# Pacing row gathers by the landing of earlier ones instead of by memsets

## The reference

```python
# 1  edge sum over the weighted edges, then a linear layer
agg = segment_sum(f[src] * w[:, None], dst);  x += agg @ W.T + b
# 2  top-1 routing to 8 experts (relu feed-forward, capacity per expert)
# 3  linear layer first, then the edge sum over the same edges turned around
h = f @ W;  agg = segment_sum(w[:, None] * h[dst], src)
x += relu(batch_norm(agg + bias) * gamma + beta)
# 4  graph attention with 4 heads over the second edge list gives scores of
#    4 experts per node; top-2 softmax mixes 4 gelu feed-forward experts
alpha = segment_softmax(leaky_relu(a_src[src] + a_dst[dst]), dst)
scores = layer_norm(segment_sum(h[src] * alpha, dst) + b_gat).mean(heads)
```

## Time and profile before

| | |
|---|---|
| three runs | 8183.62, 8189.40, 8189.93 us; median 8189.4 |
| profiled execution | span 8556.1 us, first to last instruction; no time outside the span is given for it |
| busy share of the span | PE 67%, DVE 53%, ACT 44%, POOL 68% |
| DMA | 797.56 MB, 93 GB/s over the span |
| gathers of POOL | 1563 + 1563 + 1122 in the three parts |

### The profile page before, as it was taken

The page is one execution under the profiler, slowest core; times in us unless marked ns, Lnnn a source line. Parts: engine busy times, 40 slices in busy tenths (PEclk is TensorE's granted clock), DMA queues, the critical chain, the costliest instruction groups (busy, mean ns, idle before and its releaser), DMA issues. The chain is left out here.

```text
span 8556.1 us, 91570 instructions
## 1 busy us (share of the span) xinstructions
PE 5764.1 (67%) x19687; PEld 3851.9 (45%) x19687; DVE 4500.6 (53%) x8804; ACT 3777.5 (44%) x9645; POOL 5818.2 (68%) x7545
## 2 busy tenths in 40 slices
PE   5454555555556999968465656565556888888866
PEld 4333333333335666644243434443333555555545
DVE  5354555545456999958454454554457222222227
ACT  5555555655554222226355555555555222222213
POOL 3666666666644222226688888888886688888875
PEclk8677767676665999989666767766678999999988
DMA  7333333333332111126333333333333322222218
GB/s 227 91 90 89 90 91 91 92 91 91 91 116 81 45 50 49 46 65 206 99 90 91 91 89 91 88 91 90 88 91 129 95 59 57 56 58 55 56 47 324
DMA packets 498681, 797.56 MB, mean 93 GB/s; under 512 B 121278, under 2 KB 363563, under 8 KB 498059
## 3 DMA queue, kind: packets, MB, share of 16 engines
q0 software_dynamic: 200256, 453.47, 19.5%
q1 hardware_dynamic: 297904, 338.22, 12.2%
HBM read 595.60 MB, written 197.30 MB: 93 GB/s over the span
## 5 line engine op out<-in xcount | busy, mean ns | idle before, releaser
L1013 PE MATMUL part<-rows,spread 128*128 x6656 | 2481.5, 527 | 1990.5 <-issue 984.0
L1013 PEld LDWEIGHTS part<-rows,spread 128*128 128x128 f32 x6656 | 1613.8, 261 | 2797.6 <-issue 2539.6
L970 DVE TENSOR_TENSOR agg<-agg,part 128x257 f32 (+1 forms) x3328 | 1405.1, 422 | 2230.5 <-PE part L1013 721.7
L953 POOL DMA_INDIRECT rows<-f,row x1563 | 1549.6, 991 | 733.8 <-issue 453.0
L1037 ACT ACTIVATE spread<-iota,place 128x128 f32<-128x128 f32 x3328 | 1016.1, 387 | 2038.2 <-PE part L1013 1309.5
L953 POOL DMA_INDIRECT rows<-h,row x1563 | 1550.5, 992 | 258.4 <-issue 256.3
L1952 POOL DMA_INDIRECT rows<-gat,src x1122 | 1077.9, 961 | 185.0 <-issue 185.0
L1043 ACT ACTIVATE spread<-spread,weight 128x128 f32<-128x128 f32 x3328 | 1017.5, 388 | 14.1 <-ACT spread L1039 0.3
L2030 PE MATMUL y_ps<-agg,hid 128*128 128x256 f32 x3136 | 765.4, 405 | 190.7 <-DVE y_all L2160 190.7
L2030 PEld LDWEIGHTS y_ps<-agg,hid 128*128 128x128 f32 x3136 | 640.9, 206 | 342.2 <-DVE y_all L2160 209.5
L404 POOL COPY spare<-pay 128x1024 f32<-128x1024 f32 x105 | 222.3, 2117 | 735.7 <-DVE pay L391 505.7
(11 more groups left out here) (400 smaller groups left out, 6449.2 us busy)
## 6 DMA issues: line engine op xcount, KB each, us to landing
expert_rows<-y_all SPq DMA_DIRECT2D x196, 256.0 KB
made<-expert_rows SPq DMA_DIRECT2D x49, 1024.0 KB
x<-x SPq DMA_DIRECT2D x42, 896.0 KB
rows<-f,row POOLq DMA_INDIRECT x1563
rows<-h,row POOLq DMA_INDIRECT x1563
rows<-gat,src POOLq DMA_INDIRECT x1122
xbuf<-zero SPq DMA_DIRECT2D x16, 1024.0 KB
x<-xbuf SPq DMA_DIRECT2D x32, 512.0 KB
```

The lines of the kernel that those rows point to most:

```text
L953: pool.indirect_dma_start(out=rows[:, u, 0:D], out_offset=None, in_=table, in_offset=bass.IndirectOffsetOnAxis(ap=q.row[:, i:i + 1], axis= ...
L970: nc.vector.tensor_tensor(sum_t, sum_t, part[:, p % NB, 0:WIDE], ALU.add).then_inc(added, 1)
L1013: nc.tensor.matmul(part[:, p % NB, 0:WIDE], spread[:, p % (2 * BANKS), :], row_p, start=True, stop=True).then_inc(multiplied, 1)
```

## The change

A new constant, `AFLOAT = 3`. In both edge sums the memsets and their semaphore go, and from gather 3 on each gather waits until the third gather ahead of it has landed. In the attention the memsets go as well; a gather's semaphore is now chosen by its number, `gathered[i % 3]`, a gather waits for the landing of the one three ahead, and DVE, before a block, waits on all three semaphores. The waits for `freed` stay.

```diff
+AFLOAT = 3
@@ aggregate_edges
-        worded, rested = s.sem("worded"), s.sem("rested")
+        worded = s.sem("worded")
@@
                     if i >= SPAN and u % BANKS == 0:
                         pool.wait_ge(freed, (i - SPAN) // BANKS + 1)
-                    if not begun:
-                        if i:
-                            pool.wait_ge(rested, i)
-                        nc.gpsimd.memset(k.zero[:, 0:3 * P // 2], 0.0).then_inc(rested, 1)
+                    if i >= AFLOAT:
+                        pool.wait_ge(gathered[(i - AFLOAT) % SPAN], (i - AFLOAT) // SPAN * 16 + 16)
                     pool.indirect_dma_start(out=rows[:, u, 0:D], ...)
@@ attend
-        gathered = [s.sem(f"gathered{n}") for n in range(3)]
+        gathered = [s.sem(f"gathered{n}") for n in range(AFLOAT)]
@@
                     for j in range(B):
+                        i = b * B + j
+                        if i >= AFLOAT:
+                            pool.wait_ge(gathered[i % AFLOAT], i // AFLOAT * 16)
                         pool.indirect_dma_start(out=rows[b % 3][:, j, :], out_offset=None, in_=table,
-                                                in_offset=at(src[:, b * B + j:b * B + j + 1])).then_inc(gathered[b % 3], 16)
-                        if b or j:
-                            pool.wait_ge(rested, b * B + j)
-                        nc.gpsimd.memset(rest[:, :], 0.0).then_inc(rested, 1)
+                                                in_offset=at(src[:, i:i + 1])).then_inc(gathered[i % AFLOAT], 16)
@@
-                    dve.wait_ge(gathered[b % 3], (b // 3 + 1) * B * 16)
+                    for n in range(AFLOAT):
+                        dve.wait_ge(gathered[n], len(range(n, (b + 1) * B, AFLOAT)) * 16)
```

More of the change, by code:

```diff
@@ L1909, in attend @@
         fix_i, spot_i = s.sb("fix_i", [P, 1], I32), s.sb("spot_i", [P, 1], I32)
-        begun, rest = s.sb("begun", [P, GROWS], F32), s.sb("rest", [P, 2 * P], F32)
+        begun = s.sb("begun", [P, GROWS], F32)
         rows = [s.sb(f"rows{n}", [P, B, GROWS], F32) for n in range(3)]
@@ L1933, in attend @@
         ft_in, y_out = [s.sem(f"ft_in{h}") for h in range(2)], [s.sem(f"y_out{h}") for h in range(3)]
-        gathered = [s.sem(f"gathered{n}") for n in range(3)]
+        gathered = [s.sem(f"gathered{n}") for n in range(AFLOAT)]
         stored = [s.sem(f"stored{n}") for n in range(2)]
-        spared, rested = s.sem("spared"), s.sem("rested")
+        spared = s.sem("spared")
         own, chain, freed, shifted, exped, made, tail_done, tail_turned, tail_exp, tail_exped, joined_done, carried, row_in, row_exp, row_exped, row_done, row_out = (
```

## The result

The changed kernel takes 7860.93 us (median of 4 runs, 7856.37 to 7864.25) against 8189.15 us for the kernel before, measured beside it (4 runs, 8183.62 to 8189.93): a ratio of 0.9597, 95% interval 0.9585 to 0.9609, or 328 us less. The direction was forecast.

A forecast was written before the change was run, and what follows sets the result against it. POOL's gathers were taken to bind the attention, and PE, ACT and DVE both edge sums. 8556.1 - 217 = 8339 us profiled; from the 8189.4 us runs, 7972 whole or 7981 scaled, so 7975, range 7930 to 8220.

The forecast's parts named there:

- Without interruption 1563 of them would take 1954: First edge sum: gathers at a pitch of 1.25 us would take 1954 us of a stretch of 2275.
- Step 1: Attention: memsets between gathers go, pitch falls from 1.4545 to 1.261 us, gain 217 us, at most 284.
- step 3: All three stretches: 4239 waits for the landing three gathers ahead, taken to cost 0.
- Step 2: Second edge sum: memsets go, POOL saves 216 us of time in which it ran ahead; gain taken as 0, at most 30.
- A stretched gather doesn't change that: Landing waits: a long gather delays its successors on POOL as much as itself, so landings stay some 1.25 us old.
- landings come late, and the loop of three sets the pitch: Rival, new waits of edge sums and attention: pitch 1.50 us at 4.5 us per loop, 161 us slower, 8350; 16%.
- The rule against it: Landing waits: the skill page's 2 us HBM latency at high load would make a landing 4.3 us, so waits bind.
- Step 4: Attention: DVE waits on three semaphores a block instead of one, 66 more waits; covered, or 1 us if uncovered.
- More: the second edge sum follows too: Rival: gathers bind in the second edge sum without the profiler; 30 us more gain, at most some 90, 7880 to 7945; 6%.

The follow-up runs named there:

- the second trace: The kernel before, unchanged, profiled a second time: 8190.52 us, span 8188.8 us.

## Why the prediction was wrong, step by step

**What bounds the kernel.** The reading of the attention was right, that of the edge sums wrong. "So both edge sums run at the pace of PE, ACT and DVE" rests on the earlier trace rows, which show the disturbed execution alone, and of PE's wait only the part that its records could name (51.6 us there, 1725.1 in the second trace). "Without interruption 1563 of them would take 1954" took the median gather of 0.946 us; their mean is 0.999 us, and with the 0.304 between them that gives the 2037 us of the undisturbed first sum.

**Step 1, memsets of the attention: right.** Forecast 217 us; alone, with its landing waits, this part gave 183, and without waits the stage shrank from 1629 to 1405, 224 us. The pitch after a bare gather is (1063.6 + 341.9) / 1122 = 1.253 us, against the 1.261 forecast. With waits it is 1.289 (1068.9 + 377.9): the missing 36 us belong to step 3. PE's stalls on y_ps fell to 58.3 / 33 = 1.8 us a block (forecast 2), DVE's wait to 472.1 / 33 = 14.3 us a block (forecast 12). POOL still sets the period, 1447 / 33 = 43.8 us.

**Step 2, memsets of the second edge sum: the step that failed.** "I take 0", with at most 30 us of gain. The working of the price was right: 1563 x (0.274 + 0.164 - 0.300) = 216 us, and the stage lost 2238 - 2041 = 197 without waits. What was wrong was "but of time in which it ran ahead": in the undisturbed execution no gather of this sum waits for a free bank, and PE waits for the rows. POOL's own lines had it: the "2236 of 2305 us" that the prediction added up for POOL and gave to a rival match the 2238 us that the stage takes undisturbed. So POOL bound the stage, and the memsets' time came out of it. With its waits the part gave 161 us of time. That is more than the whole miss of 114 us, since the landing waits of the other two stretches, at 0 in the sum, take some of it back.

**Step 3, the landing waits: small, not nothing.** Taken at 0, they cost 78 us by the ratios and 90.5 us by idle time. The usual case was read nearly rightly: 2.4 to 2.5 us is the time to the data, and the count on the semaphore, which the wait looks at, comes at 2.8, so a usual landing is 1.0 us old and not 1.25 when the third gather behind it is due. That is still clear of three gathers. The tail was left out. 158 of the 4239 waits stop POOL, which binds in all three stretches, so each stop counts whole: 112 stops of 63 us that go with late landings, as far as the trace has them, and 46 of 26 us at the regular places. "A stretched gather doesn't change that" holds: of the 108 stops in the edge sums only 5 waited for a gather of over 1.05 us. The latest landing is one of the attention, whose fourth gather stood 3.33 us for the landing of the first. The restart was sized at 0.43 us; in the trace with two ahead it is 0.61 from the last of a gather's DMA records to the start of the gather that waited, and 0.26 from the count on the semaphore (medians over the gaps above 0.4 us in the first sum). (2.5 + 0.61) / 3 = 1.04 is still below 1.25, so the rival "landings come late, and the loop of three sets the pitch" fails as a pitch; its late landings are there as a tail.

**The rule against it.** The latency under load that the Trainium skill names ("DMA: Bandwidth & Descriptors", Latency and other measured facts) would, by the prediction's estimate, give 4.3 us for a landing. The trace after has, for the edge sums, from issue to landing:

```profile
DMA to landing us min/median/max: 2.6/2.8/5.0
```

This view counts to the semaphore, for the gathers whose landing the trace has; in the second trace of before it gives 2.6/2.8/4.9. So the usual landing is the same before and after, and only the slowest come near 4.3 us or pass it. For the sum the trace's latency was right; whether the late ones are what the page calls high load, no run here shows.

**Step 4**: DVE's wait at L2120 shrank, so the two further waits ahead of it don't show; they were not tested alone.

**The time terms.** The sum began at 8556.1, 367 us above the runs, and the two terms were reconciled by saying that the profiler adds them. A profile of the kernel after, 7862.5 us of span, is within 0.1% of its timed median, and so is the second one of before: the profile adds nothing there, and the 367 us belong to the one disturbed execution. "More: the second edge sum follows too" came nearest to it, at 6% and with "at most some 90" of the 171 us by which that stage shrank.

The parts close the account, by stage lengths of the second trace of before and of after: first sum +29 (2037 to 2066), second -171 (2238 to 2067), attention -182 (1629 to 1447), together -324 of the 328 us measured. Against the forecast of 214 (8189 to 7975), the second sum gave 171 more and the two other terms 64 less (182 instead of 217, and 29 lost in the first sum), which makes 107 of the miss of 114.

## What to carry to other kernels

When a profiled execution is several per cent longer than the timed runs, find out where before reading what binds: look for long idle time of PE, DVE or ACT put down to "issue" or "remote", which can be waits whose records are missing, and for instructions without data whose longest time is many times their median; if there is any, profile again. A list of waits is no measure of a wait then. Here the sum of POOL's own lines, 2236 us in a stretch of 2305, said more than the list. Between back-to-back gathers on POOL, work that fits into the gap that stands there anyway is free, and everything above it is paid at every gather if POOL binds. A throttle by landings needs as many in flight as the late ones want, not the usual one: here four cost nothing that the runs can tell, three 1% and two over 16% of the time without any.

## What the runs showed of the hardware

POOL leaves 0.304 us between two gathers of 128 rows; a one-column memset of 0.12 us disappears in it, and a satisfied wait does too. A gather's landing is counted 2.8 us after its start (median), and a gather that had to wait for it sets out 0.26 us after the count, 0.61 after the last DMA record. With three in flight, POOL was stopped at every 82nd gather of both edge sums and at every 111th of the attention; where the trace has the landing, it was there already in 11 of 12 cases. In one of the traces, and in none of the others, the instructions with which SP counts landed rows took up to 1398 ns instead of 17, and the edge sums were longer by 238 and 67 us. Why, what delays single landings to 3.6 to 5.0 us, and what stops the regular gathers, stays open.
